# The absolute value in an SBUF tile, and the product with v one unit ahead of the difference

## The reference, cut to what matters

```
f1 = haar2d(x)
acc = 0
for i in range(2):
    f3 = f1 * v[i]
    f4 = einsum('bchw,oc->bohw', f3, conv_w[i])
    f5 = sign(f4) * relu(abs(f4) - tau[i])
    acc = acc + f5
y = haar2d(acc, inverse=True) + x
```

## Time and profile before

| | us |
|---|---|
| median of 3 runs (6832.41 to 6836.76) | 6836.3 |
| the profiled execution, its own time | 6835.24 |
| its span from first to last instruction | 6833.4 |
| PE, PEld busy | 6388.9, 5800.8 |
| DVE, ACT, POOL busy | 4433.1, 3968.3, 2698.2 |

### The profile page before, as it was taken

How to read it: one execution, slowest core, us unless ns; L and a number is a source line. 1 busy time by engine, 2 the same in 40 slices (tenths; PEclk the granted TensorE clock), 3 DMA queues, 4 the chain that set the end, 5 groups by cost and what they waited for, 6 DMA issues and landing times.

```text
span 6833.4 us, 144168 instructions
## 1 busy us (share of the span) xinstructions
PE 6388.9 (93%) x41056; PEld 5800.8 (85%) x41056; DVE 4433.1 (65%) x7037; ACT 3968.3 (58%) x5913; POOL 2698.2 (39%) x2052
## 2 busy tenths in 40 slices
PE   8998999889998899988999889998899988999689
PEld 7987999779997799977999779997799977998579
DVE  3667646676566764677646776567765677656766
ACT  1568545675456754567545775457654576545865
POOL 0149311483115831167311673117631176311852
PEclk9999999999999999999999999999999999999999
DMA  6654666546664466644666446664466644665236
GB/s 222 126 139 138 123 168 132 141 129 130 169 132 141 126 130 167 132 146 122 131 167 132 147 121 131 167 132 145 122 130 169 131 149 119 131 173 125 80 86 129
DMA packets 621293, 944.27 MB, mean 138 GB/s; under 512 B 62358, under 2 KB 456759, under 8 KB 621208
## 3 DMA queue, kind: packets, MB, share of 16 engines
q1 hardware_dynamic: 547480, 808.74, 51.3%
q10 hardware_dynamic: 73728, 134.25, 5.3%
HBM read 673.92 MB, written 268.83 MB: 138 GB/s over the span
## 4 chain that ended last, share of the span: by engine, by line
PE 75%; DVE 10%; ACT 8%; issue 3%; DMA 2%; POOL 1%; DVEq 1%; SPq 0%; ACTq 0%; POOLq 0%
PE ps L359 26%; PE ps L361 13%; PE ps L387 7%; PE ps L379 7%; PE ps L464 7%; PE ps L416 7%; PE ps L370 6%; DVE work L767 4%; DVE ps L782 4%; ACT ps L601 4%; ACT mag L598 4%; DMA work<-in_x_pix 1%; POOL mag L844 1%; PE ps L337 1%; DMA coef<-work 0%
## 5 line engine op out<-in xcount | busy, mean ns | idle before, releaser
L359 PE MATMUL ps<-work 128*128 128x256 f32 x8192 | 2455.2, 382 | 23.9 <-POOL work L833 16.3
L361 PEld LDWEIGHTS ps<-work 128*128 128x128 f32 x8192 | 1561.8, 191 | 214.3
L361 PE MATMUL ps<-work 128*128 128x128 f32 x8192 | 1578.0, 274 | 0.0
L359 PEld LDWEIGHTS ps<-work 128*128 128x128 f32 x8192 | 1315.8, 192 | 121.5 <-issue 20.7
L833 POOL COPY work<-field 128x512 f32 (+1 forms) x512 | 312.8, 614 | 2308.6 <-DVE ps L731 1623.3
L844 POOL TENSOR_TENSOR mag<-mag,sgn 128x1024 f32<-128x1024 f32 x512 | 1091.8, 2132 | 331.9 <-ACT mag L598 315.6
L862 POOL TENSOR_TENSOR split_a<-field,split_a 128x512 fp32r<-128x512 f32 x512 | 650.8, 1271 | 1418.8 <-ACT split_a L616 1418.8
L782 DVE TENSOR_TENSOR ps<-ps,tau_t 128x1024 f32<-128x1024 f32 x512 | 631.2, 1233 | 313.0 <-ACT ps L601 313.0
L569 ACT ACTIVATE work<-ps 128x512 f32<-128x512 f32 x512 | 306.1, 598 | 874.0 <-PE ps L361 871.1
L616 ACT ACTIVATE split_a<-field 128x512 fp32r (+1 forms) x512 | 322.9, 631 | 698.9 <-PE ps L379 694.6
L767 DVE TENSOR_TENSOR work<-ps,v_t 128x1024 f32<-128x1024 f32 x512 | 622.3, 1215 | 92.9 <-PE ps L464 92.9
(11 more groups left out here) (76 smaller groups left out, 9942.9 us busy)
## 6 DMA issues: line engine op xcount, KB each, us to landing
work<-filt SPq DMA_DIRECT2D x2048, 128.0 KB, 4.0
work<-in_x_pix SPq DMA_DIRECT2D x256, 512.0 KB, 5.4
coef<-work ACTq DMA_DIRECT2D x512, 256.0 KB, 2.1
out<-work SPq DMA_DIRECT2D x512, 256.0 KB, 4.1
rows<-in_x_rows SPq DMA_DIRECT2D x128, 512.0 KB, 4.4
mag<-in_x_rows SPq DMA_DIRECT2D x128, 512.0 KB, 4.4
rows<-coef SPq DMA_DIRECT2D x128, 512.0 KB, 3.6
split_a<-coef SPq DMA_DIRECT2D x64, 512.0 KB, 3.7
```

The lines of the kernel that those rows point to most:

```text
L359: nc.tensor.matmul(o_ps, src[:, 0, H * half:H * half + H], tab[:, N - 1::-1], start=True, stop=False)
L361: mm = nc.tensor.matmul(o_ps[:, H:N], src[:, 1, H * half:H * half + H], tab[:, N - 1:H - 1:-1], start=False, stop=True)
```

## The change

The absolute value no longer goes back into the banks but to a new tile `size`, in the part of `work` that lies behind `held` and was unused. The difference with tau works in place in `size`, and the relu reads `size`. With that the banks are free as soon as the product with v has read them, and TensorE waits on `c_scaled` in place of `c_relu`. On VectorE the product with v comes first, then the difference of the unit before, then the sum into `field`. On ScalarE the absolute value now comes ahead of the relu and has one more wait, on the relu of two units before, which reads the same half of `size`.

```diff
+        size = work[:, 6144:8192].rearrange("p (b n) -> p b n", b=2)
...
                     src = crows[(d // 2) % 4]
-                    pe.wait_ge(c_relu, 64 * b + 8 * u + d - 1 + CR)
+                    pe.wait_ge(c_scaled, 64 * b + 8 * u + d - 1 + CR)
...
                 def shrink(q, j, on):
                     u = 64 * b + 4 * q + j
+                    if on[0]:
+                        act.wait_ge(c_scaled, u + 1 + CR)
+                        act.wait_ge(c_relu, u - 1 + CR)
+                        nc.scalar.activation(size[:, j % 2], held[:, j % 2], ACT.Abs).then_inc(c_abs, 1)
                     if on[1]:
                         d = (j - 1) % 2
                         act.wait_ge(c_less, u - 1 + 1 + CR)
                         act.wait_ge(c_pair, u - 1 - 1 + CR)
-                        nc.scalar.activation(mag[:, d], banks(d), ACT.Relu).then_inc(c_relu, 1)
-                    if on[0]:
-                        act.wait_ge(c_scaled, u + 1 + CR)
-                        nc.scalar.activation(banks(j % 2), held[:, j % 2], ACT.Abs).then_inc(c_abs, 1)
+                        nc.scalar.activation(mag[:, d], size[:, d], ACT.Relu).then_inc(c_relu, 1)
+                    if on[0]:
                         act.wait_ge(c_mult, u - 1 + CR)
                         nc.scalar.activation(sgn[:, j % 2], held[:, j % 2], ACT.Sign).then_inc(c_sign, 1)
...
                     if on[0]:
                         dve.wait_ge(c_mm, u + 1 + CR)
                         dve.wait_ge(c_sign, u - 1 + CR)
                         nc.vector.tensor_tensor(held[:, j % 2].rearrange(grouped, x=4, h=4),
-                                                banks(j % 2).rearrange(grouped, x=4, h=4), table(v_t), ALU.mult)\
+                                                banks(j % 2).rearrange(grouped, x=4, h=4), table(v_t, j), ALU.mult)\
                             .then_inc(c_scaled, 1)
+                    if on[1]:
+                        d = j - 1
+                        less = size[:, d % 2].rearrange(grouped, x=4, h=4)
+                        dve.wait_ge(c_abs, u + CR)
+                        nc.vector.tensor_tensor(less, less, table(tau_t, d), ALU.subtract).then_inc(c_less, 1)
                     if on[3]:
                         ...
                                                 ALU.add).then_inc(c_field, 1)
-                    if on[0]:
-                        less = banks(j % 2).rearrange(grouped, x=4, h=4)
-                        dve.wait_ge(c_abs, u + 1 + CR)
-                        nc.vector.tensor_tensor(less, less, table(tau_t), ALU.subtract).then_inc(c_less, 1)
```

More of the change, by code:

```diff
@@ L758, in shrink, with table @@
                     grouped = "p (x c h) -> p x c h"
-                    def table(t):
-                        at = t[:, j % 2, bass.ds(2 * q + j // 2, 1), :].rearrange("p o (x h) -> p (o x) h", h=4)
+                    def table(t, d):
+                        at = t[:, d % 2, bass.ds(2 * q + d // 2, 1), :].rearrange("p o (x h) -> p (o x) h", h=4)
                         return at.unsqueeze(2).to_broadcast([128, 4, C, 4])
```

## The result

The changed kernel takes 7256.2 us (median of 4 runs, 7249.3 to 7262.0) against 6835.6 us (4 runs) of the kernel before. The ratio is 1.062, with a 95% interval of 1.060 to 1.063: slower by 421 us. The profiled execution has a span of 7247.5 us.

A forecast was written before the change was run, and what follows sets the result against it. In `shrink` the loop takes 3.54 us a unit, GpSimd at least 3.46. The difference adds 1.03 us, making 4.49; 504 x 0.95 = 479 us on 6835 gives 7314, stated as 7315 us, range 6990 to 7530.

The forecast's parts named there:

- What bounded the kernel: In `shrink`, a loop through all engines at 3.54 us a unit, with GpSimd beside it needing at least 3.46.
- freeing the banks: In `shrink`, TensorE no longer waits for the relu; worth at most 0.08 us a unit, 41 us.
- The difference costs GpSimd time: In `shrink`, VectorE's difference with two SBUF inputs takes 1.03 us a unit from GpSimd; 479 us over 504 units.
- less than a full stop: Reading of L862 beside L702 at the batch ends: 0.08 us lost against 0.22 us of overlap.
- Turns: Likeliest case in `shrink`: GpSimd stands still while VectorE's difference streams; 4.49 us a unit, 7315 us, 72%.
- sharing: Rival in `shrink`: both engines slow each other by 36% of the overlap; 0.44 us a unit, 7016 us, 13%.
- The size of a turn: Difference's loss to GpSimd in `shrink`: 1.224 - 0.21 = 1.01 us streaming plus 0.02, so 1.03 us a unit.
- The order of the turns: In `shrink`, the difference gets its turn after GpSimd's product L844 and before its sum L848, and the order repeats.
- the third rival: Wrong turn in `shrink`: difference only behind L848, GpSimd also waits for the relu; 5.79 us a unit, 7969 us, 5%.
- What TensorE waits for: In `shrink`, TensorE waits 1.2 us a unit for the product with v, and no longer for the relu.
- TensorE's clock: In `shrink`, TensorE busy 74% of a unit, granted clock stays at 0.97 or more; nothing added.

The follow-up runs named there:

- The first experiment: Changed kernel, but VectorE copies tau to an unused PSUM bank once in four units and the difference reads it there; 6830.05 us against 6830.12 before, ratio 0.9999.
- the half difference: Changed kernel with VectorE's difference over only the first 512 of 1024 values; 6991.2 us, ratio 1.024.
- new order alone: Changed kernel with absolute value, difference and relu back in the banks and TensorE waiting for the relu, new order kept; 8379.2 us, one run.

## Why the prediction was right, point by point

- **What bounded the kernel.** Right in the main point: GpSimd ran within 0.1 us of the loop, so freeing the banks could bring little and a slower GpSimd would cost in full. The size was nearly right for the steady loop, 0.07 us a unit over all stages (35 of the 41 us) and 0.056 in the first. What the forecast left out is the start of each stage, where 26 of these 35 us were spent again.
- **The difference costs GpSimd time.** Right. The first experiment takes away one of the two SBUF inputs, adds only a short copy, and the whole loss is gone. That both engines wait, whoever comes second, is shown by the rows at 448.68 and 452.84. The Trainium skill's rule ("SBUF — State Buffer", section "Who interferes with whom") holds here: the second one stands still until the first is done. The trace adds that 0.13 us at its start are free. My reading of the earlier trace rows as less than a full stop was wrong; the 0.14 us that were free are the start of GpSimd's own instruction.
- **Turns, not sharing.** Right, and the half difference shows it, 6991 us against 6989 for turns and 7050 for sharing. The share that the prediction had, 0.44 us a unit, is also half of what was measured.
- **The size of a turn.** This is the term that was off: 1.03 us, measured 0.85 (2.12 - 1.27). From GpSimd's end to the difference's end it is 1.07 us, so of the instruction's 0.21 us of fixed time, which were subtracted, 0.14 lay beside GpSimd's product (1.21 - 1.07). Not subtracted were GpSimd's own gap of 0.08 and its free 0.13 us, which lie beside the difference. That makes 1.07 - 0.08 - 0.13 = 0.86 us. A unit is 4.31 us instead of 4.49. By whole stages, from the starts of the first matrix product and of the first and last GpSimd product in all eight: the 63 steps sum to 2185 us against 1795 before (4.34 and 3.56 a step), 390 us more, and GpSimd's first step comes 9.5 to 13.9 us behind the first matrix product instead of 8.3 to 8.6, 30 us more in sum. Together 420, where the span grew by 414. The forecast had 479 for the steps and nothing for the starts. The late start hid a third of the error of the turn, and so far it was luck that the total came within 59 us.
- **The order of the turns.** Right in 494 of 504 meetings: the difference gets its turn between GpSimd's product and sum. In the other 10, as at 452.72, it comes behind the sum and the next product stands still (3.1 us), but the relu for that product is then already done, so the dear case of the third rival does not arise. What was not forecast is why it comes there: VectorE's sum into `field` waits 1.3 us for GpSimd's sum, and from there it is 0.69 and 1.22 us to the next difference.
- **What TensorE waits for.** Wrong in the detail. It was to wait 1.2 us a unit for the product with v; it waits 1.0 us in the mean and 1.2 at most ahead of `copies` (L477) for VectorE's sum (42.3 us in 41 waits), since VectorE stands in GpSimd's wait.
- **TensorE's clock.** Right in seven batches, where `shrink` shows 0.98 to 1.00, and wrong in the last. The busy time of its `shrink`, columns as in the earlier trace rows:

```profile
6700.00:6978.00 278.00, 176.87 (x728) 130.45 (x727) 191.84 (x187) 190.92 (x188) 268.29 (x129) 0.84 0.20 57
```

0.84 granted against 0.97, a mean of stretches at 1.2 and at 2.4 GHz. It costs nothing that can be seen, because GpSimd is busy 268 of these 278 us and the 63 steps take 272.4 us, against 273.2 in the others.

## What to carry to other kernels

Before a VectorE operand is moved from PSUM to SBUF, count its SBUF inputs and look at what GpSimd does at that time. With two of them, and GpSimd at work on SBUF tensors, GpSimd lost 0.86 us here for each VectorE instruction of 1.22 us, and the VectorE rows hardly show it. A short meeting elsewhere in the trace, with a control next to it, was enough to price this before the change to within 0.2 us. Where an input is small, like a table, it can go to PSUM instead, for 0.23 us in four units here.

## What the hardware showed that was not expected

- A GpSimd instruction with SBUF inputs that comes second stands still until VectorE's instruction with two SBUF inputs ends, except for its own first 0.13 to 0.14 us, with VectorE at 64, 512 and 1024 elements alike. In reverse VectorE's row lengthens up to 2.99 us and ends 1.07 us after GpSimd.
- TensorE needed 3.05 us for a unit with GpSimd's work cut, where its busy time in the kernel before was 3.32 a unit.
- The granted clock fell to means of 0.82 (new order alone, 2.1 to 2.3 us idle ahead of each product shown) and 0.84 (last batch of the changed kernel), both switching between 1.2 and 2.4 GHz; the last batch of the kernel before had 0.97. What decides between the two levels these rows do not show.
